# New orders for four engines in the first group of a conditional residual block, whose last batch is multiplied in native fp32

## The chip, the cores and the metric

The kernel runs on one core of a Trainium2 chip. The metric is the device time of one execution in microseconds (us). TensorE (PE) multiplies, VectorE (DVE) and ScalarE (ACT) copy, subtract and apply functions, GpSimd (POOL) prepares small tables, and SyncE (SP) issues transfers. ScalarE also issues some transfers on a queue of its own. Each engine runs its own list of instructions in order, and they wait for one another by semaphores.

## The reference

The input x is 64 batches of 128 rows of 512 numbers, all in fp32. Each batch has a category (of 64) and an expert (of 16). Two residual layers are computed:

```python
y = x + (x @ W[cat] + b[cat])
h = gelu(y @ fc1_w.T + fc1_b)
shared = h @ fc2_w.T + fc2_b
expert = h @ experts_w[e].T + experts_b[e]
out = y + concatenate([shared, expert])
```

W[cat] is 512 by 512, fc1_w 2048 by 512, fc2_w 384 by 2048, and an expert's matrix 128 by 2048.

## The kernel before

**Split products.** TensorE takes fp32r operands in one pass, at reduced precision. So the kernel splits each operand into a high part (a cast to fp32r, by ScalarE) and a low part (the whole less the high part, by VectorE), and adds three products: high by high, high by low, low by high. The names follow: `w_high` (L527) and `w_low` for the L0 weights, `x_high` (L534), `y_high` (L539), `prep_high` (L566) and their `_low`. All subtractions are recorded at L650, in the helper `minus`.

**Groups.** The 64 batches are taken in 16 groups of four. For a group, L0 (x by W[cat]) takes 16 slices, `l0_slice(G, j)` (L890): slice j is the k-th quarter of the contraction of batch j // 4, three matmuls of 512 columns. After the fourth slice of a batch `y_sum` (L685) adds x and puts out y. The second layer takes 16 steps c: `fc1(g, c)` (L898) is 12 matmuls into `ps_h` or `ps_e` for 128 hidden units of all four batches, then `gelu` (L573), its split (`h_high` L732, `h_low`), the split of the experts' columns (`turn_e` L713, `e_high` L559, `e_low`), `copy_last` (L725), and `fc2(g, c)` (L930), 12 matmuls into the four banks `ps_out`. In each step of group g the L0 slices of group g+1 are done too.

**Group 0** is different, since nothing ran before it. Its x is loaded whole and turned on TensorE (`turn_x`, L836), as are y (`turn_y`) and the weights of fc1 and fc2 (`turn_prep(t)`, 28 tiles of 128 by 512, then `prep_high(t)` and `prep_low(t)`). Seven of these tiles are turned before the steps have settled, two in each step from c=2. PREP is the list that says which tile is which. `fc1_ahead(c, ...)` multiplies the first three batches of step 0 or 1 while the fourth is still on its way; `fc1(0, c)` then does only the rest, 12 matmuls of 128 columns. The order in which each engine does all this is written out by hand, once per engine, ahead of its `body`. An engine that waits for a step holds up all that is listed behind it.

Slots and banks tie the lists together. The weights of L0 have eight slots in group 0, so that SP's `load_first_w(j)` waits for `w_low(j - 8)`; the split weights have five, so that `w_high(j)` waits for slice j - 5. A bank of PSUM is used in turn by x, y and prep tiles, and the waits in `turn_x`, `turn_y` and `turn_prep` guard that.

**The L0 bias** is added by one matmul for each batch (L884), whose weights pick the batch's category from a table `b0_halves`: its rows 0 to 63 are the high parts of the 64 biases, rows 64 to 127 their low parts. GpSimd makes it from the table loaded twice (L511, L513). Its matmul stands in the fourth slice of each batch.

`WHOLE` is the number of last batches of group 0 whose L0 product is done without splitting, with plain fp32 operands. The code for it is there and unused:

```python
                if whole(G, b):
                    last = nc.tensor.matmul(l0_bank(G, b)[:, :], four(x_whole_t)[:, k, :], w_slot(G, j),
                                            start=k == 0, stop=k == KD - 1)
```

With it `x_high` copies the turned x unsplit, and `w_high`, `w_low` and `x_low` are not called for that batch. The warm-up matmuls `keep_busy` (L938) also have plain fp32 operands.

## Time and profile before

| | |
|---|---|
| median of 3 runs | 1617.79 us (1616.95 to 1619.89) |
| the profiled execution | 1618.83 us |
| its span, first to last instruction | 1617.0 us |
| granted TensorE clock | 1.00 |
| busy: PE, DVE, ACT, POOL | 1597.9, 1314.5, 554.6, 4.0 us |
| matmuls | 7106 |

A row of the timeline has the start in us, the time from first start to last end, the engine, the line, the operation, output and inputs with their shapes, how many instructions are merged, and in brackets the idle time before it and what ended it. The time of several merged instructions includes overlap, since matmuls are pipelined. A row of grouped instructions has the busy time and, in ns, the mean of one. A window row gives busy time and count of each engine in a stretch, then the granted clock, the busy share of the 16 DMA engines and the GB/s they moved. SPq and ACTq are transfers issued on SyncE's and ScalarE's queues. Tiles that live in the same memory share names: `w2e` and `e_blocks` also hold split and raw L0 weights in group 0, `w` is the split fc1 weight or the table that picks categories, and `y` also holds the bias table.

### The profile page before, as it was taken

Reading aid. Unit: us, or ns where it says so; the run is one execution under the profiler, and the core shown is the slowest. Engines: PE = TensorE matmul, PEld = TensorE weight load, DVE = VectorE, ACT = ScalarE, POOL = GpSimd, SP = SyncE. Lnnn points to the kernel's source line nnn. Section 1 sums busy time; section 2 is a strip of 40 time slices with the busy share of each in tenths; the row PEclk is TensorE's granted clock in tenths of the full one; section 3 lists DMA queues with packets and bytes.
Section 4 is the critical chain, followed back from the end, with each engine's and each line's share of the span. In section 5 each row is a group of like instructions: output and inputs, shape, how many; then the busy total and the mean of one; then the engine's idle time right before and its main releaser. Section 6 shows DMA issues by size and latency. Waiting matters only on the chain.

```text
span 1617.0 us, 28052 instructions
## 1 busy us (share of the span) xinstructions
PE 1597.9 (99%) x7106; PEld 1320.7 (82%) x7106; DVE 1314.5 (81%) x2193; ACT 554.6 (34%) x926; POOL 4.0 (0%) x12
## 2 busy tenths in 40 slices
PE   7999999999999999999999999999999999999999
PEld 5887888888888888888878888888888888888887
DVE  5988879788788888878788788887888888888865
ACT  4443333333333333333333333333333333333321
POOL 0000000000000000000000000000000000000000
PEclk9999999999999999999999999999999999999999
DMA  7765555455555555555555554555545545555410
GB/s 229 198 186 157 146 159 168 135 164 144 149 166 150 154 146 151 158 157 154 142 146 150 160 160 139 163 147 149 165 145 157 147 140 167 164 149 148 136 53 27
DMA packets 303474, 243.69 MB, mean 151 GB/s; under 512 B 34324, under 2 KB 235156, under 8 KB 303380
## 3 DMA queue, kind: packets, MB, share of 16 engines
q1 hardware_dynamic: 256484, 205.57, 45.0%
q10 hardware_dynamic: 46896, 37.25, 7.3%
q14 instruction: 82, 0.67, 0.1%
q8 instruction: 12, 0.20, 0.0%
HBM read 210.18 MB, written 32.51 MB: 150 GB/s over the span
## 4 chain that ended last, share of the span: by engine, by line
PE 92%; DVE 0%; issue 0%; DVEq 0%
PE ps_out L930 41%; PE ps_e L898 21%; PE ps_h L898 21%; PE ps_y L890 10%; DVE w2e L650 0%; DVE resid L744 0%; DVE w_split L650 0%; PE ps_t L836 0%; DVE w2e L725 0%; DVE h L650 0%; DVE h L732 0%; DVE x_t L650 0%; DVEq L58 0%; DVE y L685 0%
## 5 line engine op out<-in xcount | busy, mean ns | idle before, releaser
L930 PE MATMUL ps_out<-w2e,h 128*128 128x512 f32 x3072 | 737.1, 390 | 1.5 <-DVE h L650 1.5
L930 PEld LDWEIGHTS ps_out<-w2e,h 128*128 128x128 f32 x3072 | 575.6, 188 | 121.3 <-DVE h L650 2.1
L898 PE MATMUL ps_h<-y_t,w 128*128 128x512 f32 (+1 forms) x1548 | 370.3, 388 | 0.0
L898 PE MATMUL ps_e<-y_t,w 128*128 128x512 f32 (+1 forms) x1548 | 370.2, 388 | 0.0
L898 PEld LDWEIGHTS ps_e<-y_t,w 128*128 128x128 f32 x1548 | 289.5, 188 | 59.5
L898 PEld LDWEIGHTS ps_h<-y_t,w 128*128 128x128 f32 x1548 | 289.4, 188 | 59.3
L559 ACT CAST w2e<-e_whole 128x512 fp32r<-128x512 f32 x256 | 158.8, 620 | 351.7 <-DVE e_whole L713 351.7
L713 DVE STREAM_TRANSPOSE e_whole<-e_blocks 128x512 f32<-128x512 f32 x256 | 277.0, 1082 | 0.0
L732 DVE CAST h<-g_raw 128x512 fp32r<-128x512 f32 x256 | 108.5, 424 | 161.5 <-ACT g_raw L573 158.8
L527 ACT CAST w_split<-w_raw 128x512 fp32r<-128x512 f32 x244 | 144.8, 620 | 188.9 <-DMA w_raw<-in_L_cond_W 99.3
L890 PE MATMUL ps_y<-w_split,x_t 128*128 128x512 f32 x732 | 187.9, 391 | 4.3 <-DVE w_split L650 4.1
L650 DVE TENSOR_TENSOR w2e<-e_whole,w2e 128x512 fp32r<-128x512 f32 x256 | 175.2, 684 | 17.7 <-ACT w2e L559 17.7
L650 DVE TENSOR_TENSOR h<-g_raw,h 128x512 fp32r<-128x512 f32 x256 | 177.2, 692 | 8.4
L650 DVE TENSOR_TENSOR w_split<-w_raw,w_split 128x512 fp32r<-128x512 f32 x244 | 158.7, 686 | 26.3 <-ACT w_split L527 25.8
L573 ACT ACTIVATE g_raw<-ps_e,b 128x512 f32<-128x512 f32 x128 | 88.1, 689 | 246.3 <-PE ps_e L898 222.3
L890 PEld LDWEIGHTS ps_y<-w_split,x_t 128*128 128x128 f32 x732 | 136.3, 188 | 34.9 <-issue 4.1
L573 ACT ACTIVATE g_raw<-ps_h,b 128x512 f32<-128x512 f32 x128 | 88.2, 689 | 172.6 <-PE ps_h L898 133.4
L725 DVE CAST w2e<-w2e 128x512 fp32r<-128x512 f32 x256 | 104.9, 410 | 0.0
L665 DVE STREAM_TRANSPOSE x_whole_t<-x_blocks 128x512 f32<-128x512 f32 x60 | 64.0, 1066 | 25.4 <-DMA x_blocks<-in_x 25.4
L678 DVE STREAM_TRANSPOSE w_raw<-x_blocks 128x512 f32<-128x512 f32 x30 | 33.0, 1099 | 26.0 <-DMA x_blocks<-y_rows 25.7
L534 ACT CAST x_t<-x_whole_t 128x512 fp32r<-128x512 f32 x60 | 37.2, 621 | 48.0 <-DVE x_whole_t L665 47.9
L685 DVE TENSOR_TENSOR y<-ps_y,x_raw 128x512 f32<-128x512 f32 x60 | 41.5, 692 | 5.4
(88 smaller groups left out, 427.8 us busy)
## 6 DMA issues: line engine op xcount, KB each, us to landing
e_blocks<-in_L_cond_experts_w SPq DMA_DIRECT2D x1024, 64.0 KB, 2.6
w_raw<-in_L_cond_W SPq DMA_DIRECT2D x248, 256.0 KB, 3.9
out<-resid SPq DMA_DIRECT2D x64, 256.0 KB, 2.1
x_blocks<-in_x SPq DMA_DIRECT2D x240, 64.0 KB, 2.5
b_all<-in_L_cond_b SPq DMA_DIRECT2D x60, 256.0 KB, 4.2
x_raw<-in_x SPq DMA_DIRECT2D x60, 256.0 KB, 4.8
y_rows<-y ACTq DMA_DIRECT2D x60, 256.0 KB, 3.8
x_blocks<-y_rows ACTq DMA_DIRECT2D x240, 64.0 KB, 2.8
```

Source lines behind the costliest of these rows:

```text
L527: nc.scalar.copy(split_slot(G, j)[:, 0, :], w_slot(G, j)).then_inc(w_hi, 1)
L559: nc.scalar.copy(experts_of(c % 2, 0), e_whole[:, :].rearrange("p (q v n) -> p q v n", q=GB // 2, v=2))\
L573: nc.scalar.activation(g_raw[:, c % 2, :], h_bank(c)[:, :], ACT.Gelu, bias=b1[:, c:c + 1])\
L650: return nc.vector.tensor_tensor(dst, whole, high.bitcast(F32), ALU.subtract)
L665: nc.vector.transpose(split_of(x_whole_t[:, :]), blocks_of(x_blocks[:, :])).then_inc(x_turned, 1)
L685: nc.vector.tensor_tensor(y[:, b, :], l0_bank(G, b)[:, :], resid[:, b, :] if first(G) else x_raw[:, :], ALU.add)\
L713: nc.vector.transpose(e_whole[:, :].rearrange("p (a q) -> p a q", q=Q), src).then_inc(e_turned, 1)
L725: nc.vector.tensor_copy(ring[:, c % 2, :, :, 1, :], w2[:, :, c, SHARED - P:].unsqueeze(2).to_broadcast([P, 2, GB // 2, P]))\
L732: nc.vector.tensor_copy(h[:, c % 2, 0, :], g_raw[:, c % 2, :]).then_inc(h_hi, 1)
L890: last = nc.tensor.matmul(l0_bank(G, b)[:, :], x_halves(G, b)[:, a, k, :], split_slot(G, j)[:, w, :], start=(k == 0 and n == 0), stop=(k = ...
L898: last = nc.tensor.matmul(h_bank(c)[:, at * S:end * S], w1[:, w, k, c * P:(c + 1) * P], y_t[:, a, k, at:end, :].rearrange("p b s -> p (b s)"),
L930: last = nc.tensor.matmul(ps_out[b][:, :], h[:, c % 2, a, b * S:(b + 1) * S], fc2_columns(c, c % 2, w, b), start=(c == 0 and n == 0), stop ...
```

## The change

Constants and banks. One batch of group 0 is unsplit; in PREP the fc1 tile 1 goes from place 1 to place 4, and y of batch 1 is turned in `ps_out[2]`.

```diff
     S0SLOTS = 5
-    WHOLE = 0
+    WHOLE = 1
     SPLIT = GB - WHOLE
...
         b0_table = y[:, GB - 1, :]
-        b0_high = w2e[:, W2_SIZE - 2 * D:W2_SIZE - D]
         b0_halves = w2e[:, W2_SIZE - D:W2_SIZE]
         row_of = w1[:, 1, KD - 1, HID - GB * P:HID]
-        half_sign = row_sign[:, 0:1]
         category_no = row_sign[:, 4:5].bitcast(I32)
...
         b0_high_ready = sem("b0_high_ready")
+        b0_low_in = sem("b0_low_in")
         row_of_ready = sem("row_of_ready")
         category_no_ready = sem("category_no_ready")
-        half_sign_ready = sem("half_sign_ready")
         b0_ready = sem("b0_ready")
...

-        PREP = ([("fc1", m) for m in range(2)] + fc2_tiles(0) + [("fc1", m) for m in range(2, 6)] + fc2_tiles(1)
+        PREP = ([("fc1", 0)] + fc2_tiles(0) + [("fc1", m) for m in range(1, 6)] + fc2_tiles(1)
                 + [("fc1", m) for m in range(6, 10)] + fc2_tiles(2) + [("fc1", m) for m in range(10, 14)]
...

-            return ps_y if b == GB - 1 else ps_e
+            return (ps_e, ps_out[2], ps_e, ps_y)[b]
```

SyncE's queue. One half of the bias table and the load of exps leave the head; x(2), the prep tiles and the expert blocks are interleaved anew.

```diff
               .then_inc(first_cats_in, 16)
-            for at in (0, NCAT):
-                sp.dma_start(b0_table[at:at + NCAT, :], l0_b[:, :]).then_inc(b0_table_in, 16)
-            sp.dma_start(exps[:, :], exp_ids.rearrange("(o n) -> o n", o=1)).then_inc(exps_in, 16)
+            sp.dma_start(b0_table[0:NCAT, :], l0_b[:, :]).then_inc(b0_table_in, 16)
             sp.wait_ge(cats_in, 16)
-            first_cats = []
-            for j in range(NC):
-                if j % KD == 0:
-                    first_cats.append(category(0, j // KD))
+            first_cats = [category(0, 0)]
+            for j in range(KD):
                 load_first_w(j)
-                if j == 7:
-                    load_first_x(2)
-                if j == 9:
-                    load_prep(sp, 0)
-                if j == 11:
-                    load_first_x(3)
+            sp.dma_start(exps[:, :], exp_ids.rearrange("(o n) -> o n", o=1)).then_inc(exps_in, 16)
+            first_cats.append(category(0, 1))
+            load_first_x(2)
+            load_first_w(4)
+            load_first_w(5)
+            first_cats.append(category(0, 2))
+            load_first_w(6)
+            load_first_w(7)
+            load_first_w(8)
+            first_cats.append(category(0, 3))
+            load_prep(sp, 0)
+            load_first_w(9)
+            load_first_w(10)
+            load_first_w(11)
+            load_first_x(3)
             load_prep(sp, 1)
             sp.wait_ge(exps_in, 16)
-            first_experts = []
-            for b in range(GB):
-                first_experts.append(index(exps, b, exp_w.shape[0]))
-                load_experts(0, 0, first_experts, [b])
-                if b > 0:
-                    load_prep(sp, b + 1)
-            for t in range(QUAD + 1, OWN_PREP + PSLOTS):
-                load_prep(sp, t)
+            first_experts = [index(exps, 0, exp_w.shape[0])]
+            load_first_w(12)
+            load_prep(sp, 2)
+            load_prep(sp, 3)
+            load_first_w(13)
+            load_first_w(14)
+            load_first_w(15)
+            load_experts(0, 0, first_experts, [0])
+            first_experts.append(index(exps, 1, exp_w.shape[0]))
+            first_experts.append(index(exps, 2, exp_w.shape[0]))
+            load_experts(0, 0, first_experts, [1])
+            first_experts.append(index(exps, 3, exp_w.shape[0]))
+            load_prep(sp, 4)
+            load_prep(sp, 5)
+            load_experts(0, 0, first_experts, [2])
+            load_experts(0, 0, first_experts, [3])
+            load_prep(sp, 6)
+            load_prep(sp, 7)
```

GpSimd loses the making of `b0_halves`, and ScalarE's queue gets the other half of the table.

```diff
                 .then_inc(category_no_ready, 1)
-            nc.gpsimd.memset(half_sign[0:NCAT, :], 0.0)
-            nc.gpsimd.memset(half_sign[NCAT:P, :], -1.0).then_inc(half_sign_ready, 1)
-
-            pool.wait_ge(category_no_ready, 1)
-            pool.wait_ge(half_sign_ready, 1)
-            pool.wait_ge(b0_table_in, 32)
-            nc.gpsimd.tensor_scalar(b0_high, b0_table, half_sign, None, ALU.mult).then_inc(b0_high_ready, 1)
-            pool.wait_ge(b0_high_ready, 1)
-            nc.gpsimd.tensor_tensor(b0_halves, b0_high.bitcast(F32), b0_table, ALU.add).then_inc(b0_ready, 1)

...
                 act.dma_start(resid[:, b, :], x[b, :, :]).then_inc(first_x_in[b], 16)
+            act.dma_start(b0_table[NCAT:P, :], l0_b[:, :]).then_inc(b0_low_in, 16)
             act.dma_start(b1[:, :].rearrange("p (u c) -> p u c", c=QUAD), fc1_b.rearrange("(u p c) -> p u c", p=P, c=QUAD))\
```

ScalarE's order ahead of the body, and its step 0.

```diff
             x_high(0, 0)
-            w_high(0, 0)
-            w_high(0, 1)
+            act.wait_ge(b0_table_in, 16)
+            act.wait_ge(b0_low_in, 16)
+            nc.scalar.copy(b0_halves, b0_table).then_inc(b0_high_ready, 1)
+            for j in range(0, 3):
+                w_high(0, j)
             x_high(0, 1)
-            for j in range(2, 6):
+            for j in range(3, 7):
                 w_high(0, j)
-            y_high(0, 0)
-            w_high(0, 6)
-            w_high(0, 7)
             x_high(0, 2)
-            w_high(0, 8)
-            w_high(0, 9)
+            for j in range(7, 11):
+                w_high(0, j)
+            y_high(0, 0)
+            w_high(0, 11)
             y_high(0, 1)
             prep_high(0)
-            w_high(0, 10)
-            w_high(0, 11)
             x_high(0, 3)
-            w_high(0, 12)
-            w_high(0, 13)
             y_high(0, 2)
-            w_high(0, 14)
-            w_high(0, 15)
             prep_high(1)
-            y_high(0, 3)
             prep_high(2)
-            prep_high(3)
-            prep_high(4)
+            y_high(0, 3)
+            for j in range(3, 6):
+                prep_high(j)
             act.wait_ge(b1_in, 16)
...
                             x_high(g + 1, b)
+                    if first(g) and c == 0:
+                        gelu(g, c)
+                        e_high(g, c)
+                        prep_high(6)
+                        continue
                     e_high(g, c)
...
                     gelu(g, c)
-                    if first(g) and c == 0:
-                        prep_high(5)
-                        prep_high(6)
                     for n in range(PREP_RATE):
```

VectorE's order, and its step 0.

```diff
             x_low(0, 0)
-            w_low(0, 0)
-            w_low(0, 1)
+            dve.wait_ge(b0_high_ready, 1)
+            minus(b0_halves[NCAT:P, :], b0_table[NCAT:P, :], b0_halves[NCAT:P, :]).then_inc(b0_ready, 1)
+            for j in range(0, 4):
+                w_low(0, j)
             x_low(0, 1)
-            for j in range(2, 5):
+            for j in range(4, 7):
                 w_low(0, j)
             y_sum(0, 0)
-            w_low(0, 5)
-            w_low(0, 6)
-            y_low(0, 0)
             w_low(0, 7)
...
             w_low(0, 10)
-            y_low(0, 1)
-            prep_low(0)
+            y_low(0, 0)
             w_low(0, 11)
-            x_low(0, 3)
-            w_low(0, 12)
+            prep_low(0)
+            y_low(0, 1)
             y_sum(0, 2)
-            w_low(0, 13)
-            w_low(0, 14)
-            y_low(0, 2)
-            w_low(0, 15)
             prep_low(1)
+            y_low(0, 2)
             y_sum(0, 3)
-            y_low(0, 3)
             prep_low(2)
-            prep_low(3)
-            turn_e(0, 0)
-            prep_low(4)
+            y_low(0, 3)
+            for j in range(3, 6):
+                prep_low(j)

...
                             result(g - 1, b)
+                    if first(g) and c == 0:
+                        h_high(g, c)
+                        turn_e(g, c)
+                        h_low(g, c)
+                        e_low(g, c)
+                        prep_low(6)
+                        turn_e(g, c + 1)
+                        continue
                     e_low(g, c)
...
                     h_low(g, c)
-                    if first(g) and c == 0:
-                        prep_low(5)
-                        prep_low(6)
                     if c + 1 < NC:
```

TensorE's waits for banks, its order, and its steps 0 and 1.

```diff
                 if b > 1:
-                    pe.wait_ge(x_lo, x_lows(0, b - 1))
+                    pe.wait_ge(x_lo, x_lows(0, b - 2))
                 turn(x_bank(b), [every_fourth(resid[:, b, :], k) for k in range(KD)]).then_inc(x_turned, 1)
...

-                after(pe, y_lo, b)
+                after(pe, y_lo, b - 1)
                 turn(y_bank(b), [every_fourth(y[:, b, :], k) for k in range(KD)])\
...
                     pe.wait_ge(prep_in[t % PSLOTS], 16 * (len(prep_earlier(t)) + 1))
-                if t == GB - 1:
-                    pe.wait_ge(x_lo, GB)
+                if t == 2:
+                    pe.wait_ge(y_lo, 2)
+                elif t == GB - 1:
+                    pe.wait_ge(x_hi, GB)
                 elif t == GB:
...
             keep_busy(4)
-            for j in range(5):
+            for j in range(0, 3):
                 l0_slice(0, j)
-            turn_y(0)
-            l0_slice(0, 5)
-            l0_slice(0, 6)
             turn_x(2)
+            for j in range(3, 7):
+                l0_slice(0, j)
+            turn_y(0)
             l0_slice(0, 7)
-            l0_slice(0, 8)
             turn_prep(0)
+            l0_slice(0, 8)
             turn_y(1)
...
             turn_x(3)
+            turn_prep(1)
             l0_slice(0, 11)
             l0_slice(0, 12)
-            turn_y(2)
-            l0_slice(0, 13)
-            l0_slice(0, 14)
-            l0_slice(0, 15)
-            turn_prep(1)
-            fc1_ahead(0, range(KD // 2))
-            turn_y(GB - 1)
             turn_prep(2)
-            fc1_ahead(0, range(KD // 2, KD))
+            turn_y(2)
             turn_prep(3)
+            for j in range(13, NC):
+                l0_slice(0, j)
+            fc1_ahead(0, range(KD // 2))
+            turn_y(3)
             turn_prep(4)
-            fc1_ahead(1, range(KD))
+            fc1_ahead(0, range(KD // 2, KD))
+            turn_prep(5)

...
                 for c in range(NC):
-                    fc1(g, c)
-                    if first(g) and c == 0:
-                        turn_prep(5)
+                    if first(g) and c == 1:
+                        fc1_ahead(c, range(KD))
                         turn_prep(6)
+                    fc1(g, c)
                     turn_prep(prep_in_step(g, c, 0))
```

## Rows read from the trace of the kernel before

**Rows 1.** The page's part 4, shares of the chain that ended last, by engine

```profile
PE 92%; DVE 0%; issue 0%; DVEq 0%
```

**Rows 2.** Windows, busy us (x count) of PE, PEld, DVE, ACT, POOL; clock, DMA, GB/s

```profile
7.60:34.30 26.70, 17.70 (x76) 12.25 (x77) 17.33 (x26) 12.60 (x23) 2.64 (x2) 1.00 0.77 245
...
46.00:58.00 12.00, 10.72 (x51) 8.69 (x51) 11.59 (x20) 5.20 (x10) 0.00 (x0) 1.00 0.81 202
...
128.00:1597.00 1469.00, 1467.35 (x6469) 1212.97 (x6468) 1207.22 (x2018) 496.30 (x824) 0.00 (x0) 1.00 0.51 147
```

**Rows 3.** Timeline of PE, group 0 up to the steps

```profile
9.31 0.93 PE L890 MATMUL ps_y<-w_split,x_t 128*128 128x512 f32 x3 [1.72 <-DVE w_split L650]
...
17.46 0.96 PE L890 MATMUL ps_h<-w_split,h 128*128 128x512 f32 x3 [1.09 <-DVE w_split L650]
...
25.26 0.97 PE L890 MATMUL ps_y<-w_split,x_t 128*128 128x512 f32 x3 [1.70 <-DVE w_split L650]
...
32.11 0.98 PE L890 MATMUL ps_h<-w2e,h 128*128 128x512 f32 x3 [1.22 <-DVE w2e L650]
...
45.78 2.96 PE L930 MATMUL ps_out<-w2e,h 128*128 128x512 f32 x12
...
55.97 0.72 PE L836 MATMUL ps_t<-ident,prep_raw 128*128 128x128 f32 x4 [1.28 <-DVE w L650]
```

**Rows 4.** The chain in order of time, one step in the middle of the kernel

```profile
152.43 2.72 PE ps_e L898 x12
```

**Rows 5.** Timeline of PE: warm-up matmuls, a turned prep tile, an ahead-part of fc1

```profile
6.53 1.06 PE L938 MATMUL ps_h<-ident 128*128 128x128 f32 x8
...
39.57 0.64 PE L836 MATMUL ps_out<-ident,g_raw 128*128 128x128 f32 x4
39.97 2.36 PE L898 MATMUL ps_h<-y_t,w 128*128 128x384 f32 x12
```

**Rows 6.** Timeline of ACT, group 0

```profile
7.82 1.33 ACT L527 CAST w_split<-w_raw 128x512 fp32r<-128x512 f32 x2 [1.92 <-DMA w_raw<-in_L_cond_W]
...
11.54 0.62 ACT L527 CAST w2e<-e_blocks 128x512 fp32r<-128x512 f32 x1 [0.87 <-DMA e_blocks<-in_L_cond_W]
...
15.58 0.59 ACT L539 CAST y_t<-ps_e 128x512 fp32r<-128x512 f32 x1 [2.48 <-PE ps_e L836]
...
22.89 0.59 ACT L539 CAST y_t<-ps_e 128x512 fp32r<-128x512 f32 x1 [2.34 <-PE ps_e L836]
...
30.23 0.59 ACT L539 CAST y_t<-ps_e 128x512 fp32r<-128x512 f32 x1 [1.87 <-PE ps_e L836]
```

**Rows 7.** Groups of equal shape from 0 to 46 us: busy us, mean ns, idle before

```profile
L650 DVE TENSOR_TENSOR w2e<-w_raw,w2e 128x512 fp32r<-128x512 f32 x4 | 2.6, 678 | 0.0
...
L527 ACT CAST w2e<-w_raw 128x512 fp32r<-128x512 f32 x4 | 2.3, 621 | 0.0
```

**Rows 8.** Timeline of POOL and DVE from 7 to 11 us

```profile
7.39 1.57 POOL L511 TENSOR_SCALAR w2e<-y,row_sign 128x512 fp32r<-128x512 f32 x1 [5.30 <-DMA y<-in_L_cond_b]
...
8.47 2.40 DVE L650 TENSOR_TENSOR w_split<-w_raw,w_split 128x512 fp32r<-128x512 f32 x2 [1.85 <-ACT w_split L527]
...
9.04 1.29 POOL L513 TENSOR_TENSOR w2e<-w2e,y 128x512 fp32r<-128x512 f32 x1
```

**Rows 9.** Timeline of SP, transfers issued in group 0

```profile
1.56 1.21 SPq L442 DMA_DIRECT2D y<-in_L_cond_b  x2
...
4.34 1.92 SPq L375 DMA_DIRECT2D w_raw<-in_L_cond_W  x4
...
29.48 2.67 SPq L420 DMA_DIRECT2D e_blocks<-in_L_cond_experts_w  x4
...
32.67 0.43 SPq L338 DMA_DIRECT2D x_raw<-in_L_cond_fc_w  x1
```

**Rows 10.** Windows, as in rows 2: the transfers of the first 20 us

```profile
5.00:10.00 5.00, 3.04 (x19) 2.35 (x17) 2.48 (x4) 2.67 (x5) 2.53 (x2) 1.00 0.98 282
...
15.00:20.00 5.00, 3.76 (x18) 2.59 (x17) 2.68 (x5) 2.69 (x6) 0.00 (x0) 1.00 1.02 373
```

More of the change, by code:

```diff
@@ new lines, in _ @@
+            sp.wait_ge(cats_in, 16)
+            first_cats = [category(0, 0)]
+            for j in range(KD):
+                load_first_w(j)
+            sp.dma_start(exps[:, :], exp_ids.rearrange("(o n) -> o n", o=1)).then_inc(exps_in, 16)
+            first_cats.append(category(0, 1))
[6 more added lines that the diff above has]
+            load_first_w(8)
@@ L768, in _ @@
             w_low(0, 10)
+            y_low(0, 0)
+            w_low(0, 11)
+            prep_low(0)
             y_low(0, 1)
-            prep_low(0)
-            w_low(0, 11)
-            x_low(0, 3)
-            w_low(0, 12)
             y_sum(0, 2)
-            w_low(0, 13)
-            w_low(0, 14)
+            prep_low(1)
             y_low(0, 2)
-            w_low(0, 15)
-            prep_low(1)
             y_sum(0, 3)
+            prep_low(2)
             y_low(0, 3)
-            prep_low(2)
-            prep_low(3)
-            turn_e(0, 0)
-            prep_low(4)
+            for j in range(3, 6):
+                prep_low(j)
             def body(g, more):
@@ L945, in _ @@
             keep_busy(4)
-            for j in range(5):
+            for j in range(0, 3):
+                l0_slice(0, j)
+            turn_x(2)
+            for j in range(3, 7):
                 l0_slice(0, j)
             turn_y(0)
-            l0_slice(0, 5)
-            l0_slice(0, 6)
-            turn_x(2)
             l0_slice(0, 7)
+            turn_prep(0)
             l0_slice(0, 8)
-            turn_prep(0)
             turn_y(1)
```

14 lines of the change are left out of this document (6 added, 8 removed).

## The prediction

> **What bounds the kernel now.** I read the chain that ended last first: it is TensorE for 92% of the span [rows 1]. The windows say where TensorE is not full: from 128 to 1597 us it is busy 1467.35 of 1469.00 us, from 7.6 to 34.3 us only 17.70 of 26.70 [rows 2]. So the middle is at its matmul rate, and the change touches only group 0 up to the end of step c=1. Whatever TensorE reaches earlier there moves the rest, and the end, by as much.
>
> Next I read TensorE's timeline there: the slices of L0 start at 9.31 us, the first fc2 step (12 matmuls into ps_out) at 45.78, that is 36.5 us [rows 3]. TensorE's own work between the two, by spacings of starts: 12 matmuls of 512 columns take 2.72 us [rows 4], so a slice of three 0.68 and a bias matmul 0.23; a turn of four transposes 0.40 (39.57 to 39.97), and 12 matmuls of 384 columns 2.36 with their tail, 2.2 without [rows 5]; from 39.97 to 45.78 lie those, two turns and the two rests of 12 matmuls of 128 columns, so a rest is 1.4. 16 slices 10.9, 4 biases 0.9, 13 turns (y 4, x 2, prep 7) 5.2, the ahead-parts 4.4, the rests 2.8: 24.2 us. TensorE thus waits 12.3 us: most of it recorded idle (9.0 from 7.6 to 34.3, of which 1.7 is before the first slice), the rest the tails of interrupted pipelines (a group's rows end 0.2 to 0.3 us after the next could have started).
>
> Why, the ScalarE and VectorE timelines show. Each in-order engine has work for the next slices queued behind a step of the batch before. ScalarE idles 2.48, 2.34 and 1.87 us for turn_y(0), (1), (2) [rows 6] with w_high(6), prep and w_high(10), and w_high(14) behind them; TensorE then idles 1.09, 1.70 and 1.22 us for just these slices' low halves [rows 3]. It is a ring PE, ACT, DVE, PE and not a shortage of an engine: VectorE is busy 17.33 of 26.70 us there [rows 2].
>
> **The change, part by part.** Prices: a VectorE subtract ends after 0.68 us (next start 0.60 later), a ScalarE copy after 0.62 (0.52) [rows 7], one from PSUM after 0.59 [rows 6].
>
> *Native fp32 for batch 3.* Off VectorE: four w_low and x_low(3), 5 x 0.60 = 3.0 us. Off ScalarE: four w_high, 2.1 us; x_high(3) stays. TensorE: 12 fp32r matmuls (2.7 us) become 4 fp32 ones. No 512-column fp32 matmul is in the trace. The warm-up matmuls are fp32 and stand as two records each: 8 records of 128 columns for 4 matmuls, 1.06 us, about 0.11 a record [rows 5]. Lower end, a record at the fp32r spacing of 0.227: 0.45 us a slice. Upper end, 0.11 scaled by four: 0.88. I take 0.88, since two records for one matmul say that the operand is not taken at the fp32r rate: 3.5 us, +0.8 against before (other end -0.9). The Trainium skill ("FP8 and Floating Point Precision", TensorE Precision Notes) says true fp32 is four passes; at 0.227 a pass that would be 0.91 a slice, 0.1 us more in all.
>
> *b0_halves.* Two GpSimd operations go. They cost more than their own time: of two VectorE subtracts from 8.47 the pair took 2.40 us, where two take 0.60+0.68 = 1.28, while GpSimd ran from 9.04 to 10.33 [rows 8]; the second slice waits for the longer one. That 1.0 us is on the path and goes. The Trainium skill ("SBUF — State Buffer", SBUF: two separate sides) has the two engines' shared port pair as a lock by which the loser blocks fully. The stretched subtract agrees; the first of the pair must have ended by 9.31, when TensorE starts on its slice, though GpSimd was in its first operation from 7.39 to 8.96, so it was not held. Added instead: one ScalarE copy (0.52) ahead of w_high(0,0) and one VectorE subtract (0.60) ahead of w_low(0,0). Both table halves land before the weights in before's order (weights 0 are first cast at 7.82 [rows 6]), so these fill waiting time; without that cover they cost 0.5 each.
>
> *SP's queue.* One table half goes to ScalarE's queue and the load of exps behind the weights, which takes 0.6 us (1.21 for both halves) and an issue more from ahead of the first weights; they are issued from 4.34 on now [rows 9], then 0 (if the category's read sets it) to 1.1 us earlier. The 16 transfer engines are full from then on: 282 and 373 GB/s are 0.93 and 0.70 us a 256 KB tile [rows 10]. Weights 4 landed at 11.5 [rows 6] as the eighth tile; in the new order that place is x(2)'s, and w4 follows at 12.4, w8 near 15.8, w11 18.4, w13 22.3, w15 23.6 if nothing is gained. I take a gain of 0.5 in this curve (ends 0 and 1.1). Prep tiles 2 and 3 now land near 21, where before they were issued among the expert blocks; prep 4 and 5 are issued near 24, where 5 had 32.67 [rows 9].
>
> *The orders.* ScalarE and VectorE now run w_high/w_low up to 10 ahead of y_high(0)/y_low(0), and three turns (prep 2, y 2, prep 3) stand between slices 12 and 13. I walked the three engines: each step starts when its engine is free and its last producer has ended, at the prices above. The same walk on the kernel before gives its first fc2 34.9 us after the first slice, the trace 36.5; of the 1.6 missing, 1.0 is the GpSimd stretch, so 0.6 is what such a walk forgets. After: first slice 8.7; turn_x(2) 11.1 (waits 0.2 for its tile); slice 4 at 13.4 (waits 0.9, weights 4); slice 9 at 18.4 (0.1, w_low); from there no wait: slice 13 at 23.6, fc1_ahead at 26.4, fc1(0,0)'s rest at 29.8, first fc2 at 35.1. With the forgotten 0.6: 35.7, against 45.78. **Sum: 10.1 us.** Check by work: TensorE's own 24.2+0.8 = 25.0 us plus some 2 of waits from 8.7.
>
> What is late next: y_high(2) and (3) still stand 2.5 and 3.2 us on ScalarE for their turns, with prep casts behind, but TensorE has slices 13 to 15 and the prep turns to do. The first e_whole needs all 16 expert blocks: the walk issues the last at 28.1 and lands it at 31.8, wanted at 32.4. fc1_ahead(1) and turn_prep(6), now behind fc1(0,0), hide gelu(0) and the expert split. After c=1 no order changes; the 1.28 us idle at 55.97 (VectorE's prep_low) [rows 3] stays at 0.7 to 1.3, and I count nothing. The steps of c=1 to c=3 need SP's biases and next weights 10 us earlier too; by the walk SP has slack of about 1 us there.
>
> The profiled execution is 1618.8 us (span 1617.0), 1.0 over the median of 1617.8. 1617.8 - 10.1 = 1607.7.
>
> **The rivals.** (A, forecast) the walk holds within 2 us: 1605.7 to 1609.7.
> (B) *Supply is late*: SP is one queue with 22 tiles and 16 blocks, and a group of four expert issues took 2.67 us where four weights took 1.92 [rows 9]. For it: slacks of 0.6 and 1 us. Against: SP stands waiting in before for w_low. Two or three such slips put the expert blocks 2 to 3 us behind their use, and TensorE waits them out at fc2(0,0): gain 7, 1610.8 (1609.7 to 1613).
> (C) *More*: tiles come 1.1 us earlier, fp32 slices at the lower price and the idle at 55.97 gone: 10.1+0.5+1.2+0.8 = 12.6, 1605.2.
> (D) *VectorE takes over*: from 46 to 58 us it was busy 11.59 of 12.00 us [rows 2]; if it runs behind by the time gained, the 10 us come back as prep_low waits and the result is within 3.2 us of before: 1616.
> (E) *Slower than before*: prep tiles 4 and 5 now stand in TensorE's order ahead of fc1(0,0), and everything behind them waits. Behind turn_prep(5) the walk has 5.8 us to the first fc2, with the forgotten part 6.4. Even issued as late as before, at 32.67, and 3.5 us on the way as weights 0 (4.34 to 7.82), tile 5 gives 36.2+6.4 = 42.6, still before 45.78. The point from which it decides is a landing after 42.6, which makes 3.2 us more than before: SP's stream, which waits for w_low(4) to (7) ahead of the tile, would have to stand 14 us. Then 1622.
> (F) *Batch 3 is not run as fp32*: then its matmuls stay single records, without split operands, and TensorE saves the 0.8 us: 1606.9.
>
> **How the numbers follow.** A 0.54, B 0.21, C 0.13, D 0.07, E 0.04, F 0.01. A change of 0.2% is 3.2 us, which is about what a measurement of this kernel can tell from none. Faster: A, B, C, F, 0.89; same: D, 0.07; slower: E, 0.04. The range takes A, most of B and most of C: 1605.0 to 1612.5; 8 in 10 lie in it.
>
> **What would show it.** Right: the first fc2 group near 35.7 us; TensorE busy over 85% between its first slice and there; slices 12 to 15 as 8 records on w_raw or e_blocks; no stretched subtract near 9 us; steps from c=2 on as before, about 10 us earlier. Wrong: TensorE idle for e_blocks, prep_raw or x tiles by DMA after 20 us (B); idle for prep_low or h_low beyond 1.3 us after c=1 (D); fp32 slices spaced well below or above 0.88.

## The result and the profile after

| | before | after |
|---|---|---|
| time, median of 5 runs each, taken in turn | 1617.79 us (1616.95 to 1622.03) | 1610.05 us (1607.04 to 1611.38) |
| ratio, 95% interval | | 0.9942 (0.9928 to 0.9956) |
| profiled execution, its span | 1618.8, 1617.0 us | 1610.3, 1608.5 us |
| first fc2 group of TensorE starts at | 45.78 us | 36.52 us |

The kernel became faster by 0.58%. The ratio on 1617.8 us is a gain of 9.4 us (7.1 to 11.6), the difference of the medians 7.7, that of the two spans 8.5. The forecast was 1607.7 us with 1605.0 to 1612.5 around it. A second series of the same kernel (the control below) gave 0.9935 (0.9922 to 0.9948), 10.5 us.

The page of the kernel after, its first lines:

```profile
span 1608.5 us, 27987 instructions
PE 1597.6 (99%) x7102; PEld 1321.4 (82%) x7102; DVE 1310.7 (81%) x2189; ACT 553.8 (34%) x923; POOL 0.9 (0%) x8
```

Its windows, with the columns of [rows 2]: us, then the busy time (x count) of PE, PEld, DVE, ACT and POOL, the granted clock, the DMA share and GB/s:

```profile
7.60:26.00 18.40, 16.89 (x80) 13.63 (x81) 13.03 (x22) 11.65 (x21) 0.00 (x0) 0.91 0.98 325
26.00:38.00 12.00, 12.00 (x77) 10.69 (x76) 9.59 (x16) 4.21 (x8) 0.00 (x0) 1.00 0.82 220
36.70:48.70 12.00, 11.22 (x53) 9.11 (x53) 11.19 (x18) 5.04 (x9) 0.00 (x0) 1.00 0.78 189
128.00:1597.00 1469.00, 1467.29 (x6465) 1212.53 (x6464) 1205.16 (x2015) 496.27 (x823) 0.00 (x0) 1.00 0.51 146
```

TensorE is busy 28.89 of 30.40 us from 7.6 to 38 us; before, it was 17.70 of 26.70 up to 34.3 [rows 2]. The middle of the kernel has not moved: 1467.29 us of 1469.00 against 1467.35. The window from 36.7 us holds the steps that stood from 46.0 us on before. All of the gain arises in the first 38 us, as TensorE's timeline shows (a bracket is an idle time ahead of the row and what ended it; rows without one follow with no recorded wait):

```profile
9.11 3.08 PE L894 MATMUL ps_y<-w_split,x_t 128*128 128x512 f32 x6 [2.02 <-DVE w_split L653]
11.99 1.08 PE L894 MATMUL ps_y<-w2e,x_t 128*128 128x512 f32 x3
...
22.69 1.02 PE L890 MATMUL ps_h<-e_blocks,x_whole_t 128*128 128x512 f32 x2
...
24.98 1.88 PE L890 MATMUL ps_h<-e_blocks,x_whole_t 128*128 128x512 f32 x4
...
27.38 1.61 PE L902 MATMUL ps_e<-y_t,w 128*128 128x384 f32 x6
...
36.52 2.98 PE L934 MATMUL ps_out<-w2e,h 128*128 128x512 f32 x12
...
46.24 0.72 PE L838 MATMUL ps_t<-ident,prep_raw 128*128 128x128 f32 x4 [0.78 <-DVE w L653]
...
54.75 0.72 PE L838 MATMUL ps_t<-ident,prep_raw 128*128 128x128 f32 x4 [0.43 <-DVE w2e L653]
```

The waits of 1.09, 1.70 and 1.22 us [rows 3] are gone; between 9.11 and 46.24 us no wait of TensorE is recorded. Two things are new. The wait at 54.75 had no counterpart before (nor has it one in the control below), and the first slices are slow: six matmuls take 3.08 us here, since the granted clock stood at the lower of its two levels, 1.2 GHz, from 9.1 to 12.5 us (0.91 in the window's mean). It fell after TensorE's idle 2.02 us.

ScalarE still waits for its two late turns, and VectorE's part of the table is no longer stretched. ScalarE's rows first, then VectorE's:

```profile
6.43 0.62 ACT L591 CAST w2e<-y 128x512 fp32r<-128x512 f32 x1 [0.52 <-DMA y<-in_L_cond_b]
24.70 0.59 ACT L543 CAST y_t<-ps_e 128x512 fp32r<-128x512 f32 x1 [2.63 <-PE ps_e L838]
29.52 0.59 ACT L543 CAST y_t<-ps_y 128x512 fp32r<-128x512 f32 x1 [3.26 <-PE ps_y L838]
```

```profile
7.08 0.69 DVE L653 TENSOR_TENSOR w2e<-y,w2e 64x512 fp32r<-64x512 f32 x1 [0.45 <-ACT w2e L591]
9.79 0.69 DVE L653 TENSOR_TENSOR w_split<-w_raw,w_split 128x512 fp32r<-128x512 f32 x1 [0.83 <-ACT w_split L531]
48.82 0.56 DVE L706 TENSOR_TENSOR resid<-y,b_all 128x384 f32<-128x384 f32 x1 [0.51 <-DMA be_all<-in_L_cond_experts_b]
```

The native fp32 matmuls, grouped by their line (ns: least, median, most; first and last start):

```profile
L890 PE MATMUL ps_h<-e_blocks,x_whole_t x8: 591/592/595, 22.7 to 27.4; 128*128 128x512 f32 x8
```

Four matmuls stand as eight records; inside a group the rows start 0.43 us apart, so a slice takes 0.86 us (slice 12 starts at 22.69, the next row at 23.55).

**A mark to compare kernels by.** TensorE's turns of one prep tile are the same work in every kernel here. Their starts, and how much earlier than before (in brackets):

| turn of prep_raw | before | after | control | swap (below) |
|---|---|---|---|---|
| c=1 | 51.30 | 42.07 (9.2) | 41.45 (9.9) | 41.6 (9.7) |
| c=2 | 55.97 | 46.24 (9.7) | 45.64 (10.3) | 45.76 (10.2) |
| c=3 | 63.88 | 54.75 (9.1) | 53.68 (10.2) | 53.68 (10.2) |
| group 1, the tile with a wait | 123.96 | 114.87 (9.1) | 114.50 (9.5) | 112.99 (11.0) |
| span | 1617.0 | 1608.5 (8.5) | 1610.2 (6.8) | 1605.1 (11.9) |

Below the fourth line it is noise for this question: in the hundreds of equal steps each of these executions has one to four waits of 0.3 to 1.5 us, for h or for a low half x_t, in different places, before's too (one of 1.5). So the marks judge a part of the change, the medians the whole.

### The profile page after: what moved, and what is told of

Same layout as the page of the kernel before. It is cut to its first block and busy times, and to the rows that moved or that the text cites. A ratio compares the mean times of both kernels' runs of the same rounds, so it can differ in the third digit from the quotient of the medians.

```text
span 1608.5 us, 27987 instructions
## 1 busy us (share of the span) xinstructions
PE 1597.6 (99%) x7102; PEld 1321.4 (82%) x7102; DVE 1310.7 (81%) x2189; ACT 553.8 (34%) x923; POOL 0.9 (0%) x8
## 5 line engine op out<-in xcount | busy, mean ns | idle before, releaser
L653 DVE TENSOR_TENSOR w_split<-w_raw,w_split 128x512 fp32r<-128x512 f32 x244 | 157.8, 682 | 26.1 <-ACT w_split L531 25.8
```

The costliest lines, as they stand in the source:

```text
L653: return nc.vector.tensor_tensor(dst, whole, high.bitcast(F32), ALU.subtract)
```

## The experiments

In all short diffs the context is left out. "Kernel before" and "kernel after" are the two of the change. In the expectations, e1, e6, e7 and e9 are experiments 1, 7 (ten warm-up matmuls), 8 and 9. The runs were made in three series, and the kernel before was run again in each: its median was 1621.25 us beside experiments 1 to 4, 1619.30 beside 6, 8 and the ten warm-up matmuls of 7, and 1619.28 beside the others. So medians of different series aren't compared here; every ratio is against the kernel before of its own series.

**1. The table alone.** The kernel before, with only the new way of b0_halves.

```diff
-            for at in (0, NCAT):
-                sp.dma_start(b0_table[at:at + NCAT, :], ...)
+            sp.dma_start(b0_table[0:NCAT, :], ...)        # SP
+            act.dma_start(b0_table[NCAT:P, :], ...)       # ScalarE's queue
-            nc.gpsimd.tensor_scalar(b0_high, ...)
-            nc.gpsimd.tensor_tensor(b0_halves, ...)
+            nc.scalar.copy(b0_halves, b0_table)
+            minus(b0_halves[NCAT:P, :], ...)              # VectorE
```

> The kernel before with one part of the change alone: b0_halves made by one ScalarE copy and one VectorE subtract, half of the table loaded on ScalarE's queue, no GpSimd work after its first microseconds. Theory (the stretched subtract lies on TensorE's path, the two new operations fill waiting time): no VectorE subtract near 9 us over 0.7 us, slice 1 starts right behind slice 0, first fc2 about 1.0 us earlier than 45.78, so 44.8, and a time of some 1616.8. Rival (later waits take it back, since slice 4 waits for its weights anyway): first fc2 within 0.3 of 45.78. Rival (the copy and the subtract stand ahead of the first weights and are not hidden): first slice at 9.8 or later, fc2 46.3.

1619.24 us (1615.4 to 1623.99, 10 runs), ratio 0.9994 (0.9981 to 1.0008). The trace has the first slice at 8.82 and fc2 at 44.72: 1.06 us earlier than before. About half of it (0.49) is that the first slice starts earlier; from there to slice 2 TensorE takes 2.21 us (8.82 to 11.03) instead of 2.82 (9.31 to 12.13), since the subtract is no longer stretched. The ratio would be a gain of 1.0 us, but its interval goes from 1.3 us slower to 3.1 faster, so it tells neither a gain nor none. In the profiled execution the microsecond doesn't reach the end, as TensorE's timeline in group 1 and two windows of it show:

```profile
123.72 0.94 PE L830 MATMUL ps_t<-ident,prep_raw 128*128 128x128 f32 x4 [2.05 <-DVE w2e L642]
124.31 2.91 PE L884 MATMUL ps_y<-w_split,x_t 128*128 128x512 f32 x6
```

```profile
122.00:124.00 2.00, 0.28 (x2) 0.31 (x3) 2.00 (x5) 0.00 (x0) 0.00 (x0) 1.00 0.97 121
124.00:126.00 2.00, 2.00 (x8) 1.71 (x8) 1.89 (x3) 0.59 (x1) 0.00 (x0) 0.51 0.64 175
```

The wait there grew from 1.24 to 2.05 us, so that the turn starts only 0.24 us earlier than before. Then the granted clock is at 1.2 GHz for 3.4 us with TensorE the bound, and one step later TensorE is 1.3 us behind before (its next turn of prep_raw starts at 129.95 against 128.64): 1.5 us given back by the clock, 0.8 by the wait. A gain of 1 us at the start can be eaten by one such place.

**2. Native fp32 alone.** The kernel before, with WHOLE = 1 and the splits of batch 3 left out of both engines' orders.

```diff
-    WHOLE = 0
+    WHOLE = 1
-            w_high(0, 12) ... w_high(0, 15)
-            x_low(0, 3), w_low(0, 12) ... w_low(0, 15)
-                    pe.wait_ge(x_lo, GB)
+                    pe.wait_ge(x_hi, GB)
```

> The kernel before, in its own orders, with batch 3 of group 0 multiplied in native fp32 and its nine splitting operations gone; nothing else. Theory (the gain is of the orders; fp32 only frees VectorE and ScalarE): the waits before slices 6, 10 and at x(2) stay as they were, those of slices 12 to 15 go (about 2.5 us with their tails), TensorE pays 0.7 more; first fc2 1.5 to 2.5 us earlier, 43.3 to 44.3, time 1615.5 to 1616.3. Rival (the freed splitting work is the gain): first fc2 below 39, time 1610 or less.

1620.71 us (1614.39 to 1624.39, 10 runs), ratio 0.9996 (0.998 to 1.0012). TensorE's timeline in the walk:

```profile
17.45 0.97 PE L881 MATMUL ps_h<-w_split,h 128*128 128x512 f32 x3 [1.11 <-DVE w_split L646]
20.98 0.93 PE L881 MATMUL ps_y<-w2e,x_t 128*128 128x512 f32 x3 [1.14 <-DVE w2e L646]
25.27 0.96 PE L881 MATMUL ps_y<-w_split,x_t 128*128 128x512 f32 x3 [1.71 <-DVE w_split L646]
28.67 1.91 PE L877 MATMUL ps_h<-e_blocks,x_whole_t 128*128 128x512 f32 x2
45.31 2.96 PE L921 MATMUL ps_out<-w2e,h 128*128 128x512 f32 x12
```

The waits ahead of the slices are what they were; only those inside batch 3 are gone. fc2 starts at 45.31, 0.5 us earlier than before, and not 1.5 to 2.5 as expected. Here, too, the clock takes a part: it was at 1.2 GHz from 27.4 to 30.8 us, where two of the fp32 records take 1.91 us against 1.02. By the 3.4 us at half speed that is up to 1.7 us (an estimate), so the edit is worth 0.5 measured and at most 2.2: native fp32 alone doesn't carry the gain.

**3. All but native fp32.** The kernel after, with WHOLE = 0; the splits of batch 3 stand again among the casts of the new orders.

> The changed kernel with batch 3 split again: new orders, new queue, new table, four w_high, four w_low and x_low(3) put back between the y and prep steps. Theory (orders carry it): VectorE was busy 13.0 of 18.4 us between 7.6 and 26, so 3.0 us more fit mostly; TensorE has 0.7 us less work; weights 13 to 15, which land at 23.6 to 25.4, now need 1.4 us more through ScalarE and VectorE. First fc2 between 36.0 and 39.0, time 1609 to 1612. Rival (native fp32 carries it): first fc2 over 42.

1613.15 us (1611.51 to 1614.55, 6 runs), ratio 0.996 (0.9947 to 0.9973). TensorE's timeline:

```profile
23.24 0.93 PE L903 MATMUL ps_h<-w2e,h 128*128 128x512 f32 x3 [0.94 <-DVE w2e L657]
28.20 0.97 PE L903 MATMUL ps_h<-w2e,h 128*128 128x512 f32 x3 [1.90 <-DVE w2e L657]
38.66 2.98 PE L943 MATMUL ps_out<-w2e,h 128*128 128x512 f32 x12
```

So orders, queue and table bring 7.1 us of fc2's start, and fp32 the other 2.1 (36.52) to 2.8 (35.91 of the control). The two waits are those that the kernel after avoids. Ahead of slice 12, w_low(12) stands on VectorE behind the low halves of prep 0, y(1) and x(3); ahead of slice 14, w_high(14) stands on ScalarE behind y_high(2), which waits 1.98 us for its turn, and a prep cast.

**4. All but SP's queue.** The kernel after, with the order of transfers of before.

> The changed kernel with SP's order of before behind the table half (weights one after another, prep tiles 2 to 5 among and behind the expert blocks). Theory (the queue's order is a needed part): TensorE turns prep tile 2 between slices 12 and 13, but the tile lands near 27 to 28 as before, so TensorE stands there for some 5 us, and again for tile 4 or 5 before fc1(0,0); first fc2 at 41 to 44, time 1614 to 1618, VectorE and ScalarE idle. Rival (the transfers were hidden anyway): first fc2 within 1 us of 36.5.

1620.68 us (1618.27 to 1623.72, 10 runs), ratio 0.9997 (0.9984 to 1.001).

```profile
10.36 2.54 PE L878 MATMUL ps_y<-w_split,x_t 128*128 128x512 f32 x6 [2.44 <-DVE w_split L637]
...
30.09 1.13 PE L822 MATMUL ps_out<-ident,be_all 128*128 128x128 f32 x4 [4.47 <-DMA be_all<-in_L_cond_fc_w]
45.38 2.98 PE L918 MATMUL ps_out<-w2e,h 128*128 128x512 f32 x12
```

TensorE's new order has the turn of prep 2 ahead of slice 13, and in before's queue that tile stands behind expert blocks: 4.47 us of waiting for it, and the granted clock is at 1.2 GHz from 27.8 to 34.7 us. From slice 12 to fc2 are 20.77 us here and 13.83 in the kernel after, 6.9 of the 8.9 us by which fc2 is later than there. The other 1.9 us arose ahead of slice 12 and not by this edit alone: the first slice starts at 10.36, since the first weights are cast only at 8.88, where experiment 1, with the same head of the queue and the same time of issue, casts them at 7.29; the clock is then low from 10.9 to 14.2 us as well. That is why fc2 comes later than the 41 to 44 expected. The second wait that was expected, for tile 4 or 5, didn't come. By the ratio of ten runs, the orders without their queue are worth nothing.

**5. The queue and the table on the kernel before,** with before's orders of the engines. One execution.

> The kernel before with the new table (as e1) and the new order of SP's queue, engines' orders as before. Theory (before waited in its ring of engines, not for transfers): tiles land as in the profile after, but first fc2 within 1 us of e1's 44.7, TensorE's waits before slices 6, 8 and 10 at 1.1, 1.1 and 1.7 us as before; queue and orders pay only together. Rival (supply was the larger part): first fc2 below 41.

1619.79 us. The waits of 1.09, 1.14, 1.70 and 1.22 us stand ahead of the same slices as before, and fc2 starts at 45.21 (44.72 with the table alone; here the granted clock is at 1.2 GHz from 25.8 to 29.2 us). None of these waits goes with the queue. The time is that of a single execution and tells little. With experiments 2 to 4 the change is seen to be one thing in three parts: the orders need the tiles in their sequence, and fp32 pays more where the slices no longer wait in a ring. Not tried apart from the orders were the new places in PREP, the bank ps_out[2] for y of batch 1, and the looser waits for banks.

**6. The control.** The kernel after once more, in the series of experiment 8 and of the ten warm-up matmuls of 7.

> The changed kernel itself, as a control beside the next three. Theory: TensorE from its first slice to the first fc2 without a recorded wait of over 0.3 us, 27.4 us when the granted clock falls in it as it did in the profile after (9.1 to 12.5 us), about 26.6 when it does not. Rival (the first profile was a lucky one and TensorE waits for tiles in most): waits on weights or prep tiles appear and the first fc2 comes after 38.

1609.1 us (1608.35 to 1611.99, 5 runs), ratio 0.9935 (0.9922 to 0.9948), TensorE at 2.4 GHz throughout in the profiled execution:

```profile
8.76 1.60 PE L894 MATMUL ps_y<-w_split,x_t 128*128 128x512 f32 x6 [1.69 <-DVE w_split L653]
13.59 1.67 PE L894 MATMUL ps_h<-w_split,h 128*128 128x512 f32 x6 [0.20 <-DVE w_split L653]
15.97 0.50 PE L888 MATMUL ps_h<-w2e,w 128*128 128x512 f32 x1 [0.25 <-DVE w2e L653]
35.91 2.98 PE L934 MATMUL ps_out<-w2e,h 128*128 128x512 f32 x12
45.64 0.72 PE L838 MATMUL ps_t<-ident,prep_raw 128*128 128x128 f32 x4 [0.80 <-DVE w L653]
```

From the first slice to fc2 are 27.15 us, against 27.41 with the fallen clock of the first profile; the 26.6 expected at full clock didn't come. Slice 2 starts 1.8 us later in the first profile (11.99 against 10.21, of which 0.35 is the later first slice), but the later ones wait for their weights at full clock (0.20 and 0.25 above), so most of it is taken up.

**7. Ten warm-up matmuls instead of four** (keep_busy(4) to keep_busy(10)), against the fall at 9.1 us.

> The changed kernel with ten instead of four warm-up matmuls behind the second turn, which fill TensorE's 2.0 us idle ahead of the first slice. Theory (the idle time let the clock fall just where TensorE has become the bound, and that is the 0.8 us by which the first fc2 came later than forecast): granted clock 1.00 from 5 to 15 us, slices 0 to 2 spaced 0.7, first fc2 at 35.4 to 35.9 in place of 36.5, time 0.5 to 1 us below the control. Rival (slices 1 and 2 wait for their low halves anyway): first fc2 within 0.2 of 36.5 even at full clock.

1611.11 us (1607.95 to 1615.07, 6 runs), ratio 0.9948 (0.9933 to 0.9962). The clock held, but the warm-up runs right up to the first slice, which starts at 9.26, and fc2 at 36.42. The rival's number came true, though by the later start: from the first slice to fc2 are 27.16 us, as in the control. The reverse, without keep_busy(4):

> The changed kernel without the four warm-up matmuls behind the second turn, so TensorE is idle from about 6 to 9 us. Theory (its granted clock falls after a longer idle time, and every stretch at the lower level in which TensorE is the bound costs half of its length): a stretch or two at 0.5 between 6 and 16 us, first fc2 0.5 to 2 us later than the control's 35.9. Rival (clock does not matter there, as slices wait for weights): within 0.3 of 35.9, or no fall of the clock.

1610.2 us in one execution: idle 2.37, first slice at 8.74, 1.2 GHz from 9.4 to 12.8 us, fc2 at 36.34, 0.4 later than the control and 0.2 earlier than in the first profile of the kernel after, between theory and rival. Neither difference can be put down to the clock. The work that leads to the first fc2 stands in the same order in all kernels of experiments 6 to 10, but for the number of warm-up matmuls, and in the six profiles with full clock there (control, ten warm-up matmuls, both kernels of 8, 9 and 10) fc2 starts at 35.87 to 36.88 us, 26.97 to 27.98 us after the first slice, 27.4 in the mean; where it takes longest, TensorE waits for weights (0.60 us ahead of slice 2 in the first kernel of 8). With the fallen clock these are 27.41 and 27.60. So the clock at the start costs some tenths at most, and less than what executions differ by.

**8. Prep casts ahead of gelu and h_high in group 0**, against the waits at 45.6 and 114.5 us. The lines are shortened.

```diff
+                    prep_high(prep_in_step(g, c, 0))
                     gelu(g, c)
-                    prep_high(prep_in_step(g, c, 0))
+                    prep_low(prep_in_step(g, c, 0))
                     h_high(g, c)
-                    prep_low(prep_in_step(g, c, 0))
```

> The changed kernel with the first prep tile of each step of group 0 cast ahead of gelu and split ahead of h_high. Theory (the three waits left on TensorE's prep turns, 0.78, 0.43 and 1.16 us, come from ScalarE and VectorE taking gelu's work first, which is due only a step later): these waits go, group 1 starts 2.0 to 2.4 us earlier, time 2 us below the control. Rival (VectorE is full there, so another of its results is late instead): waits for h_low or e_low of 1 us and more in place of them, gain below 0.5.

1610.34 us (1607.32 to 1612.16, 5 runs), ratio 0.9941 (0.9928 to 0.9954). The wait at c=2 is 0.43 us instead of the control's 0.80, the one in group 1 still 1.61 (1.82 in the control). The theory fell, and VectorE's timeline of this kernel says why:

```profile
108.49 1.09 DVE L670 STREAM_TRANSPOSE x_whole_t<-x_blocks 128x512 f32<-128x512 f32 x1 [1.67 <-DMA x_blocks<-in_x]
109.50 0.65 DVE L697 TENSOR_TENSOR x_raw<-x_raw,b_all 128x512 f32<-128x512 f32 x1
110.25 0.69 DVE L690 TENSOR_TENSOR y<-ps_y,x_raw 128x512 f32<-128x512 f32 x1
...
113.59 0.68 DVE L655 TENSOR_TENSOR w2e<-ps_t,w2e 128x512 fp32r<-128x512 f32 x1
```

VectorE waits 1.67 us for a transfer of x, with add_b0, y_sum and all the low halves up to the prep tile (113.59) queued behind it. Both edits together:

> Both edits of e6 and e7. Theory: their effects add, 2.5 to 3.4 us below the control, so that it beats both kernels; granted clock 1.00 in the first 130 us. Rival: no more than the better of the two.

1608.92 us (1606.08 to 1615.63, 5 runs), ratio 0.993 (0.9917 to 0.9942); its profiled execution is the slowest of the five and has waits of 1.48 (55.83) and 1.80 us (116.40). The ten warm-up matmuls end ahead of the first slice here, which starts at 8.90 after 0.37 us of idle. More can't be told from it.

**9. add_b0 and y_sum ahead of turn_x** in group 0's preparation of group 1, so that they fill that wait.

```diff
-                            if b + 1 < GB:
+                            if b + 1 < GB and not first(g):
                                 turn_x(g + 1, b + 1)
                             add_b0(g + 1, b)
                             y_sum(g + 1, b)
+                            if b + 1 < GB and first(g):
+                                turn_x(g + 1, b + 1)
```

> The changed kernel with one swap on VectorE in group 0: add_b0 and y_sum of a batch stand ahead of the next batch's turn_x. Theory (the wait of 1.2 to 1.8 us that is left near 114.5 us in every run so far is VectorE standing 1.7 us for x blocks at turn_x(3), with add_b0, y_sum, the weights' low halves and at last prep_low behind it): that wait falls below 0.5 us, group 1 starts 0.8 to 1.4 us earlier against the forecast of the control's trace, time about 1 us below the control. Rival (the x blocks only land later, since something else is behind y_sum): wait at 114 unchanged.

1607.8 us (1604.18 to 1610.76, 6 runs), ratio 0.9931 (0.9917 to 0.9946). VectorE, then TensorE:

```profile
106.56 0.68 DVE L695 TENSOR_TENSOR x_raw<-x_raw,b_all 128x512 f32<-128x512 f32 x1
107.34 0.69 DVE L688 TENSOR_TENSOR y<-ps_y,x_raw 128x512 f32<-128x512 f32 x1
108.11 1.09 DVE L668 STREAM_TRANSPOSE x_whole_t<-x_blocks 128x512 f32<-128x512 f32 x1
```

```profile
112.99 0.72 PE L840 MATMUL ps_t<-ident,prep_raw 128*128 128x128 f32 x4 [0.34 <-DVE w2e L653]
```

The wait for x is gone, the one of TensorE is 0.34 instead of 1.82 us, and the mark is 11.0 us ahead of before where the control has 9.5. It is surely faster than the kernel before. Against the control it is 1.5 us better by the mark of one execution each, but the intervals of the ratios overlap (0.9931 against 0.9935 and 0.9942 of the kernel after), so that it is the faster one was not shown.

**10. The swap with eight warm-up matmuls.**

> The swap of e9 and eight warm-up matmuls in place of four (ten, in e6, ended after the first slice's operands were ready). Theory: first slice as in the control (8.8), clock 1.00 there, and e9's gain on top: 1 to 1.5 us below the control. Rival: same as e9 within the measurement.

1608.68 us (1607.15 to 1613.34, 6 runs), ratio 0.9937 (0.9923 to 0.995), so again nothing for the warm-up. The profiled execution is the slowest of the six, and it shows what can go wrong. VectorE and ScalarE, then TensorE, then a window:

```profile
50.17 0.56 DVE L706 TENSOR_TENSOR resid<-y,b_all 128x384 f32<-128x384 f32 x1 [2.50 <-DMA be_all<-in_L_cond_experts_b]
51.26 0.62 ACT L531 CAST w_split<-w_raw 128x512 fp32r<-128x512 f32 x1 [4.31 <-DMA w_raw<-in_L_cond_W]
```

```profile
57.11 1.10 PE L840 MATMUL ps_t<-ident,prep_raw 128*128 128x128 f32 x4 [3.43 <-DVE w2e L653]
```

```profile
55.00:60.00 5.00, 2.89 (x9) 2.53 (x10) 4.71 (x9) 2.06 (x4) 0.00 (x0) 0.59 0.80 192
```

fc2 starts at 35.87, earlier than in any other profile, and then the biases of the experts and the next weights come late: a wait of 3.43 us for TensorE, and the granted clock at 1.2 GHz from 55.9 to 62.7 us. The turn of c=3 starts at 57.11, where the control has 53.68. The same be_all wait is 0.51 us in the profile of the kernel after. SyncE's queue shows when the next weights were issued, in the kernel before, the kernel after and here:

```profile
52.92 0.92 SPq L384 DMA_DIRECT2D w_raw<-in_L_cond_W  x2
45.38 0.85 SPq L382 DMA_DIRECT2D w_raw<-in_L_cond_W  x2
45.59 1.25 SPq L382 DMA_DIRECT2D w_raw<-in_L_cond_W  x2
```

In the kernel before SyncE had issued nothing for 2.8 us ahead of them, in the kernel after for 0.5: they are issued 7.5 us earlier than before, where TensorE's turn of c=2 is 9.7 us earlier. From their issue to ScalarE's first cast are 4.9 us before and after, 4.4 in the control and 5.7 here. So most of what is worse here than in the kernel after arose in the transfers, which were issued only 0.2 us later; why they took longer no run shows.

## Why the prediction was right, and where it was off

**The path: right.** TensorE's start of the steps set the end, and the middle kept its rate.

**The walk: right within its own error.** Forecast 8.7 for the first slice and 35.7 for fc2; the control has 8.76 and 35.91, the profile of the kernel after 9.11 and 36.52. First slice to fc2 was to be 27.0 us and is 27.15 and 27.41, in the six profiles with full clock 26.97 to 27.98. Its stations, with the control's in brackets: turn_x(2) 11.1 (10.97), slice 4 13.4 (12.46), slice 9 18.4 (18.71), slice 13 23.6 (24.36), fc1_ahead 26.4 (26.76), the rest of fc1(0,0) 29.8 (30.62), fc2 35.1 (35.91). Two errors offset each other here, and that is luck. The wait of 0.9 for weights 4 doesn't come, so the first slice to slice 4 takes 3.70 us and not 4.7; 0.20 and 0.25 stand instead at slice 5 and at the bias of batch 1. From slice 4 to slice 13 it takes 11.90 us and not 10.2: beside those 0.45 us, the tails at the changes between slices and turns cost more than the 0.6 allowed for. From slice 13 to fc2 the walk's 11.5 is 11.55. ScalarE's waits for its turns came as written, 2.63 and 3.26 us for 2.5 and 3.2.

**The fp32 slice: right.** 0.88 us taken, 0.86 measured; the lower end of 0.45 is out. The rule of the Trainium skill named there ("FP8 and Floating Point Precision", TensorE Precision Notes) made 0.91, and the spacing of 0.43 for each of two records agrees with it within 6%. Its share of the gain I didn't forecast by itself; experiments 2 and 3 give 0.5 us alone and 2.1 to 2.8 with the orders. (C took 1.2 us for cheaper fp32 slices, where its own prices, 0.88 and 0.45 for four slices, make 1.7; C didn't come, so nothing hangs on it.)

**The GpSimd stretch: the mechanism right, the size not.** The subtracts near 9 us all take 0.69. But of the 1.06 us of experiment 1 the earlier first slice makes 0.49, which the walk counted apart (9.31 to 8.7), and the stretch about 0.6 where 1.0 was taken: slice 2 still waits 0.24 us for its own weights' low half. Taking away GpSimd's operations and putting the table before the weights are one edit here, so which of the two shortens the path was not tried apart.

**SP's queue: right in what it does**, and more than a term. I priced it as 0.5 us in the curve of arrivals; experiment 4 shows that without it the whole gain is gone, mainly through prep tile 2 (4.47 us of wait and the clock behind it). The text had them "land near 21" without saying what the orders would be without that.

**After c=1: the step that was off.** "I count nothing" held for the idle of 1.28 us (now 0.78, in 0.7 to 1.3), but not for what is new: VectorE waits 0.51 us for be_all (the experts' biases), ScalarE 2.73 us for weights at 50.31, and TensorE has 0.43 us of wait at 54.75. The mark falls there from 9.7 to 9.1. That is SP's slack of "about 1 us", used up: the weights are issued 7.5 us earlier where 9.7 were needed (experiment 10). What it costs differs by execution. TensorE's wait at c=3 is none in the control, in the first kernel of 8 and in 9, 0.17 us with ten warm-up matmuls, 0.43 in the kernel after, 0.90 without the four, 1.48 with both edits of 8, and 3.43 in experiment 10, there with slower transfers on top. Rival B had the place wrong (the expert blocks of fc2(0,0) came in time in every profile with the new queue and orders) but was right that supply comes next.

**The sum.** 10.1 us were forecast; fc2's start gives 9.3 and 9.9, the turn of c=3 9.1 and 10.2, the ratios 9.4 and 10.5. In the first profile 0.4 us went at the first slice, 0.4 between it and fc2 and about 0.6 at c=3, and 0.5 came in where the idle of 1.28 us shrank to 0.78. The rest down to the 8.5 of the spans lies in the middle, in the scattered waits named above. A, the likeliest case, came true; D and E did not. VectorE is as full in the same steps as it was, 11.19 of 12.00 us (from 36.7 us) against 11.59 (from 46), but TensorE's waits for its prep_low stayed at 0.78 and 0.43 us and didn't eat the gain.

**Part of the ratio may not be the path.** The clock falls after waits of TensorE. The mean granted clock over the runs was 0.9985 to 0.9987 (before, in three series), 0.9969 (experiment 4, with the longest wait), 0.9998 (control) and 0.9997 (swap). A kernel with fewer waits also loses less to the clock, which may be why the ratio of the control (10.5 us) exceeds its marks (9.5 to 10.3). That is argued from these means and was not isolated, and the interval of that ratio (8.4 to 12.6 us) is wider than the difference.

## What to carry to other kernels

Where in-order engines wait for each other in a ring, find the operation with others queued behind it, and walk the engines with measured prices; that walk gave 27.0 us where six executions took 27.0 to 28.0, with errors of up to 1.7 us in its parts that partly offset each other. Order of work and order of transfers are one edit: the orders without their queue were worth nothing by ten runs, and the queue without the orders removed none of the waits in the one execution of it. After such a gain look for the next wait that scales with it (a queue whose slack is used up, an engine that stands ahead of a late tile with work that doesn't need it), since a later wait can give back a whole microsecond.

## What the hardware showed that was not expected

- The granted clock drops to 1.2 GHz after waits of TensorE, and not in every execution of a kernel: after 2.02 us idle in the profile of the kernel after, not after 1.69 in its second profile (the control), after 2.05 in experiment 1, behind waits of 1.1 to 1.7 in experiment 2 that in the kernel before left it at 2.4 GHz. Its price is that of the place: 1.5 us where TensorE is the bound (experiment 1), too little to tell where the slices wait for weights anyway (experiment 7).
- Matmuls that keep TensorE busy against it brought nothing here: ten of them held the clock, and the first slice began 0.5 us later than in the control in one profile (9.26) and 0.1 later in another (8.90).
- Equal transfers, issued at the same time, land at different times in different executions: the first weights, issued at 3.8 us, are cast at 7.29 in experiment 1 and at 8.88 in experiment 4. No run shows why.
- A 512-column native fp32 matmul costs 0.86 us where a slice of three fp32r ones costs 0.68 [rows 4], and it takes 0.5 to 0.6 us of cast on ScalarE and 0.6 of subtract on VectorE away. By these prices it pays only while those two are on the path.
